# The expert stage of an attention and mixture-of-experts layer, with the weights as the stationary operand

## Chip, core and metric

The kernel runs on one core of one Trainium2 chip. The metric is the device time of one execution in microseconds (us). The core's engines work side by side, each through a queue of its own in program order: TensorE (PE in the profile; its weight loads are the row PEld), VectorE (DVE), ScalarE (ACT), GpSimd (POOL) and SyncE (SP), which here only issues transfers (DMAs). They wait for one another by semaphores alone. On TensorE a matmul streams the columns of its moving operand past a stationary operand, which a weight load puts in place ahead of it. `order` rows below name the output, then `<-`, the stationary or first input and the moving one.

## What is computed

The input x is 2 sequences of 2048 tokens of 256 numbers, 4096 tokens in all.

```python
def reference(x, Wq, Wk, Wv, Wo, Wg, bg, gate_w, ew1, ew2, ew3, sw1, sw2, sw3):
    x = x + layernorm(attention(layernorm(x)))       # gated linear attention, 16 heads of 16, a scan over time
    x = x + layernorm(ffn(layernorm(x)))
    return x

def ffn(x):
    top_v, top_i = top_k(x @ gate_w, 2)              # 8 experts, each token takes 2
    w = softmax of the two chosen gates, 0 elsewhere
    out = sum over experts e of swiglu(x, ew1[e], ew2[e], ew3[e]) * w[e]
    return out + swiglu(x, sw1, sw2, sw3)            # the shared expert

def swiglu(x, w1, w2, w3):                           # w1, w2: 256 x 512; w3: 512 x 256
    h = x @ w1
    return h * sigmoid(h) * (x @ w2) @ w3
```

## The kernel before

There are three parts. The **first stage** (functions `sync_a`, `tensor_a`, `vector_a`, `scalar_a`, `pool_a`) goes through the tokens in C = 16 steps of 128 tokens of both sequences: attention, the first residual (kept in DRAM as `x1_scratch`), the second norm (`xn2`) and the routing. Every step POOL scatters the rows of `xn2` four times over (2 sequences, 2 choices) by indirect DMA (`scatter`, L538 to L544) into `xs_scratch`, where each expert has a region of its own; SP also stores them in the tokens' order behind those regions (`store_xn2`, L348). The scales of the norms are made on POOL in `rstd_x`, `rstd_o` and `rstd_x1` (L516 to L535, with `ve` from the variances `mv`, `mvo`), which stand in POOL's queue among the scatters.

The **expert stage** works on tiles of 128 rows, in this order: EARLY = 12 tiles of the shared expert (which need no routing), RT = 72 routed tiles (8192 rows, and up to one part-filled tile for each of 8 experts), and 20 shared ones, the tail. Which expert a routed tile belongs to is known only on the chip: DVE writes it to a table, `tab`, and each engine loads the number of the expert from there into a register (`expert_of`, L1131; `entry`, L1128 and L1129). A weight's address is then worked out from this register. Everything is fp32 made of two f16 numbers, a high and a low part: a product is three f16 matmuls, high by high, high by low and low by high. With `xh`, `xl` for the rows, `gh`, `gl` for the gated hidden values, and `W16` for the weights.

Within a tile (`tensor_b`): `turn_x` (L1193) transposes the rows that SP loaded (`xt`); ACT makes `xh` (`high`, L1264), DVE `xl` (L1414). `hidden` (L1208) multiplies: the rows are stationary, the weights move, 512 columns at a time, 6 matmuls for `bank` of the first and 6 for the second product. ACT takes the silu (`sl`, L1270), DVE gates it (`gg`, L1425). `turn_g` (L1199) transposes `gg` in four pieces of 128x128 fp32; ACT and DVE make `gh` (L1258) and `gl` (L1407) of it. `project` (L1218) multiplies it by the down weights in 12 matmuls of 256 columns; ACT scales the result out (`yo` or `ysh`, L1282). SP stores `yo` in the order of the tiles in `ys_scratch` (L1145 to L1170). Engines run the three steps of a tile on slots that overlap: in slot t TensorE does `hidden` of tile t, the transposes of t-1 and t+1, and the down product of t-2.

**Weights.** The f32 weights of the experts arrive by DMA; DVE takes the largest absolute value of each (`largest_of`, L1350), beside the first slots (the list `beside`: a "table stage" is one entry of it), `scales` (L766) makes `w_scale` from them, and POOL then splits a whole expert in three instructions (`split` in `pool_b`: L1441, L1445, L1447) of 3072 elements a partition. Experts 0 to HEAD-1 are handled early; the others, seven of the nine with the shared one, in this way.

**Tail.** When all routed tiles are stored, POOL gathers for each step of 128 tokens of both sequences the routed results of each token (`gather`, L1475: four indirect DMAs, with `gi` copied at L1469); DVE mixes them with `ysh` by the gate's weights (`mix`: L1367, L1373; statistics at L1378 to L1387), POOL raises the variance to the power -1/2 (`rstd`, L1481), DVE makes the shift (L1393), ACT normalises (`lnc`, L1290), DVE adds x1 (`residual`), SP stores. POOL's part of this is `pool_c`, a queue of its own order: scale of step c, then gathers of c+2.

## Time and profile before

| what | us |
|---|---|
| device time, median of 3 runs (lowest to highest) | 885.7 (880.39 to 886.43) |
| the profiled execution's own time | 884.06 |
| its span on the core | 881.7 |
| TensorE busy | 779.2 (88% of the span) |
| TensorE's weight loads busy | 551.0 |
| DVE, ACT, POOL busy | 559.7, 423.7, 413.8 |
| DMA: packets, MB | 71381, 96.55 |

The span is the time from the first to the last instruction of the profiled execution, and the 2.4 us to its own time lie around it. Busy times are sums over the whole span; since the kernel has stages with other limits, they are read stage by stage, by windows and by the timeline. The page's "chain that ended last" is followed back from the last instruction to what released each. The page's course of three engines in 40 slices of 22 us (tenths of busy time; PEclk is TensorE's granted clock):

```
PE   3879888898999984899999999999999999977772
DVE  4797988897988993699433334433334433477774
POOL 3122335876777775681899960000000000377773
PEclk8899989999999997799999999999999999999996
```

The first stage takes the first 15 slices or so, the early shared tiles three more, the routed ones go on to slice 33, and the tail follows.

### The profile page before, as it was taken

Reading aid. Unit: us, or ns where it says so; the run is one execution under the profiler, and the core shown is the slowest. Engines: PE = TensorE matmul, PEld = TensorE weight load, DVE = VectorE, ACT = ScalarE, POOL = GpSimd, SP = SyncE. Lnnn points to the kernel's source line nnn. Section 1 sums busy time; section 2 is a strip of 40 time slices with the busy share of each in tenths; the row PEclk is TensorE's granted clock in tenths of the full one; section 3 lists DMA queues with packets and bytes.
Section 4 is the critical chain, followed back from the end, with each engine's and each line's share of the span. In section 5 each row is a group of like instructions: output and inputs, shape, how many; then the busy total and the mean of one; then the engine's idle time right before and its main releaser. Section 6 shows DMA issues by size and latency. Waiting matters only on the chain.

```text
span 881.7 us, 24476 instructions
## 1 busy us (share of the span) xinstructions
PE 779.2 (88%) x8205; PEld 551.0 (62%) x8205; DVE 559.7 (63%) x1195; ACT 423.7 (48%) x811; POOL 413.8 (47%) x452
## 2 busy tenths in 40 slices
PE   3879888898999984899999999999999999977772
PEld 3667667687877763466666666666666666644441
DVE  4797988897988993699433334433334433477774
ACT  2555556565666552343444444444444444444442
POOL 3122335876777775681899960000000000377773
PEclk8899989999999997799999999999999999999996
DMA  7243333443345347781111111111111212345554
GB/s 238 68 102 83 98 101 78 141 121 110 111 138 144 111 121 264 271 287 48 44 60 56 62 58 58 61 58 59 60 55 61 61 60 63 96 131 186 168 156 130
DMA packets 71381, 96.55 MB, mean 109 GB/s; under 512 B 8800, under 2 KB 58080, under 8 KB 71264
## 3 DMA queue, kind: packets, MB, share of 16 engines
q1 hardware_dynamic: 59376, 69.31, 26.5%
q0 software_dynamic: 6528, 17.83, 6.2%
q10 hardware_dynamic: 5360, 7.87, 2.7%
q8 instruction: 71, 1.16, 0.6%
q14 instruction: 46, 0.38, 0.1%
HBM read 63.25 MB, written 31.72 MB: 108 GB/s over the span
## 4 chain that ended last, share of the span: by engine, by line
PE 44%; DMA 5%; DVE 4%; issue 4%; POOL 3%; ACT 0%; POOLq 0%; SPq 0%; ACTq 0%; DVEq 0%
PE bank L1208 25%; PE bank L1218 12%; DMA ya<-ys_scratch,gi 4%; PE bank L1199 4%; PE bank L1193 2%; POOL ya L1475 2%; DVE cmb L1367 1%; DVE cmb L1373 1%; DVE stc L1378 0%; POOL xs_scratch L544 0%; DVE mvc L1384 0%; DMA xt<-xs_scratch 0%; POOL rsc L1481 0%; DVE vec L1387 0%; PE bank L741 0%
## 5 line engine op out<-in xcount | busy, mean ns | idle before, releaser
L1208 PE MATMUL bank<-W,xh 128*128 (+1 forms) x832 | 249.4, 382 | 15.3 <-DVE xl L1414 15.1
L1407 DVE TENSOR_TENSOR gl<-bank,gh 128x512 f16<-128x512 f32 x104 | 71.7, 690 | 162.9 <-ACT gh L1258 162.8
L1208 PE MATMUL bank<-W,xl 128*128 (+1 forms) x416 | 158.5, 381 | 0.0
L1218 PE MATMUL bank<-W,gh 128*128 (+1 forms) x832 | 143.4, 274 | 0.0
L1208 PEld LDWEIGHTS bank<-W,xh 128*128 128x128 f16 x832 | 80.4, 98 | 73.6 <-DVE xl L1414 19.7
L1218 PE MATMUL bank<-W,gl 128*128 (+1 forms) x416 | 114.1, 274 | 0.0
L1425 DVE SCALAR_TENSOR_TENSOR gg<-sl,w_scale,bank 128x512 f32<-128x512 f32 x104 | 77.6, 747 | 56.1 <-PE bank L1208 52.1
L1469 POOL COPY gi<-pos_all 128x4 uint32 (+1 forms) x16 | 2.9, 179 | 232.4 <-DMA ys_scratch<-yo 232.4
L544 POOL DMA_INDIRECT xs_scratch<-xn,posi x64 | 94.3, 1473 | 31.8 <-issue 23.2
L1218 PEld LDWEIGHTS bank<-W,gh 128*128 128x128 f16 x832 | 81.9, 98 | 31.8
L600 PE MATMUL bank<-xnT,wT 128*128 128x256 f32 x384 | 94.8, 399 | 0.7 <-ACT xnT L386 0.7
L1282 ACT ACTIVATE yo<-bank,w_scale 128x256 f32<-128x256 f32 x72 | 34.2, 475 | 126.3 <-PE bank L1218 126.3
L1258 ACT ACTIVATE gh<-bank 128x512 f16<-128x512 f32 x104 | 62.1, 597 | 57.4 <-PE bank L1199 57.4
L600 PEld LDWEIGHTS bank<-xnT,wT 128*128 128x128 f32 x384 | 73.0, 197 | 17.7 <-issue 5.9
L1270 ACT ACTIVATE sl<-bank,w_scale 128x512 f32<-128x512 f32 x104 | 71.5, 688 | 20.1 <-PE bank L1208 19.7
L1475 POOL DMA_INDIRECT ya<-ys_scratch,gi x64 | 67.5, 1055 | 27.0 <-POOL gi L1469 12.3
L834 DVE TENSOR_TENSOR_SCAN W<-W,diag 128x1024 f32<-128x1024 f32 x32 | 71.9, 2279 | 8.4 <-DMA W<-gate_scratch 8.3
L1199 PE MATMUL bank<-ident,gg 128*128 128x128 f32 x416 | 63.1, 274 | 14.2 <-DVE gg L1425 14.2
L1199 PEld LDWEIGHTS bank<-ident,gg 128*128 128x128 f32 x416 | 50.4, 141 | 39.2 <-issue 19.5
L1208 PEld LDWEIGHTS bank<-W,xl 128*128 128x128 f16 x416 | 40.9, 98 | 49.6 <-issue 1.1
L1441 POOL TENSOR_TENSOR wtmp_p<-W,w_scale 128x3072 f32<-128x3072 f32 x8 | 42.5, 5309 | 21.3 <-DVE w_scale L778 20.8
L704 PE MATMUL bank<-W 64*32 64x64 f32 x2048 | 35.3, 221 | 17.5 <-issue 13.8
(177 smaller groups left out, 1325.8 us busy)
## 6 DMA issues: line engine op xcount, KB each, us to landing
W<-gate_scratch SPq DMA_DIRECT2D x64, 256.0 KB, 4.8
xt<-xs_scratch SPq DMA_DIRECT2D x104, 128.0 KB, 2.0
ys_scratch<-yo SPq DMA_DIRECT2D x72, 128.0 KB, 1.7
W<-in_L_ffn_ew_dram ACTq DMA_DIRECT2D x15, 512.0 KB, 6.3
W<-in_L_ffn_ew_dram SPq DMA_DIRECT2D x9, 512.0 KB, 8.3
x_in<-in_L_attn_x_dram SPq DMA_DIRECT2D x16, 256.0 KB, 4.0
x_scratch<-x SPq DMA_DIRECT2D x16, 256.0 KB, 2.2
xs_scratch<-xn SPq DMA_DIRECT2D x16, 256.0 KB, 3.1
```

The costliest lines, as they stand in the source:

```text
L544: pool.indirect_dma_start(xs_d[:, :], bass.IndirectOffsetOnAxis(ap=posi[:, s, b * TOPK + k:b * TOPK + k + 1], axis=0), xn2[s % XB][:, b, : ...
L600: last = mm(dst[:, g * B * P:(g + 1) * B * P], wT[:, n, k, g * P:(g + 1) * P], xnT[s % 2][:, k, :], start=(k == 0), stop=(k == KC - 1))
L834: V.tensor_tensor_scan(dec[:, w, :], gbc[s % 2][:, w, :], free2(diag[:, :, :]), 0.0, ALU.mult, ALU.add).then_inc(S["decay_ready"], 1)
L1199: last = nc.tensor.transpose(pGT[:, c * P:(c + 1) * P], gg[t.side][:, c * P:(c + 1) * P], ident[:, :])
L1208: last = mm(dst[t.side][:, :], a[t.side][:, k, :], W16[:, e, m, s, k * H:(k + 1) * H], start=(n == 0), stop=(n == 3 * KC - 1))
L1218: last = mm(pYB[t.side][:, 0:D], a[t.side][:, c, :], W16[:, e, 2, s, c * D:(c + 1) * D], start=(n == 0), stop=(n == 3 * HC - 1))
L1258: act.activation(gh[u.side][:, :, :].rearrange("p c t -> p (c t)"), pGT[:, :], ACT.Copy)\
L1270: act.activation(sl[t.side][:, :], pH1[t.side][:, :], ACT.Silu, scale=w_scale[:, 0, e])\
L1407: V.tensor_tensor(gl[u.side][:, :, :].rearrange("p c t -> p (c t)"), pGT[:, :], gh[u.side][:, :, :].rearrange("p c t -> p (c t)"), ALU.sub ...
L1425: V.scalar_tensor_tensor(gg[t.side][:, :], sl[t.side][:, :], w_scale[:, 1, e], pH2[t.side][:, :], ALU.mult, ALU.mult).then_inc(T["gg_ready ...
L1441: pool.tensor_tensor(wtmp_p[:, :, :].rearrange("p m n -> p (m n)"), whole, w_scale[:, 1, e:e + 1].broadcast_to([P, 3 * MW]), ALU.mult).the ...
L1475: pool.indirect_dma_start(ya[c.side][b][k][:, :], None, ys_d[:, :], bass.IndirectOffsetOnAxis(ap=gi[c.side][:, b * TOPK + k:b * TOPK + k + ...
```

## The change

The expert stage is turned round. The weights are stationary and the rows move (`hidden`): a weight block of 128x128 meets the transposed rows of a **unit** of 256 rows. The hidden values come out transposed already, so the transposes of `gg` go (`turn_g`), and ACT and DVE take `gh` and `gl` from `gg` itself. The down product stays as it was, 12 matmuls of 256 columns for 128 rows and all of the hidden values.

A unit of 256 rows is worked through in two **halves**, each with half of the hidden columns (24 matmuls of 256 columns in `hidden`) and two chunks of the down product for its two tiles (12 matmuls of 256 columns); each half fills a slot. There are 6 early shared units (slots 0 to 11), PAIRS = 25 routed units of 256 rows (slots 12 to 61), and 21 routed **single** units of 128 rows for the rest (slots 62 to 82), each with 48 matmuls of 128 columns in `hidden`, 12 of 256 for the down product and 2 transposes. The tail begins at slot 83 with 10 shared units. RU = 46 is the number of routed units. The units of 256 rows take the first 25 full pairs of tiles in the experts' order; all other rows go to singles.

- **Shared rows.** SP stores the transposed `xn2T` of the first stage in `xT_scratch` (`store_xn2T`) in place of the rows, and the shared units load it transposed: no `turn_x` there.
- **Rows carry their destination.** A row of `xs_scratch` is DR = 272 floats, 1088 bytes: 256 of data, and the token's number and first choice, which POOL writes ahead of each step's scatters (two operations on 128x2 and a wait, `tagged`). POOL has seven more constants to make at the start. On DVE `rows_to` makes from them the row of `ys_scratch` that each result belongs to (`idx`).
- **Scatter in place of gather.** Results of routed units leave ACT into `yo` (3 buffers) and POOL scatters them to the tokens' order (`spread`, one indirect DMA for each 128 rows). `ys_scratch` is then in the tokens' order, and SP loads it for the tail with direct DMAs, two slots ahead (`load_mix`). The four gathers a step go.
- **POOL's queue.** It works slot by slot with the others: from slot SHARE + 1 = 11 on two thirds of an expert's split (`split(e, m)`, 1024 elements instead of 3072) a slot for four slots, then one, and behind them in each slot the scatter of the routed unit that ended three slots before. In the tail it takes over `low_g` (`gl`) in each slot, `low` (`xl`) every second one, and `residual`, beside the scale.
- **ACT and DVE** follow the new slots; the table stages beside the tiles on DVE are one fewer (`SHARE`).

The core of the diff:

```diff
-    EARLY = 12
-    T0 = EARLY + RT
...
+    EARLY = 6
+    PAIRS = -(-(TOPK * TOK - E * (2 * P - 1)) // (2 * P))
+    RU = PAIRS + (TOPK * TOK + E * (P - 1)) // P - 2 * PAIRS
...
-        xs_d = nc.dram_tensor("xs_scratch", [ROWS, D], F32).ap()
-        ys_d = nc.dram_tensor("ys_scratch", [RT * P, D], F32).ap()
+        xs_d = nc.dram_tensor("xs_scratch", [SPARE + P, DR], F32).ap()
+        ys_d = nc.dram_tensor("ys_scratch", [TOPK * TOK + (RU - PAIRS) * P, D], F32).ap()
+        xT_d = nc.dram_tensor("xT_scratch", [C, P, KC * B * P], F32).ap()
...
-            def store_xn2(s):
-                need(sp, S["xn2_ready"], B * (s + 1))
-                sp.dma_start(xs_by_step[s], xn2[s % XB][:, :, :]).then_inc(xs_stored[s % XB], 16)
+            def store_xn2T(s):
+                need(sp, S["xn2T_ready"], s + 1)
+                sp.dma_start(xT_d[s], free2(xn2T[s % 2][:, :, :])).then_inc(xT_stored[s % 2], 16)
...
             def scatter(s):
                 need(pool, S["pos_ready"], s // BATCH + 1)
                 need(pool, S["xn2_ready"], B * (s + 1))
+                need_dma(pool, scattered, s - XB, B * TOPK)
+                pool.tensor_scalar(xn2[s % XB][:, :, D], token2[:, :], float(TOPK * P * s), None, ALU.add)\
+                    .then_inc(tagged, 1)
+                pool.tensor_copy(xn2[s % XB][:, :, D + 1], choice_all[:, s, 0:B * TOPK:TOPK]).then_inc(tagged, 1)
+                need(pool, tagged, XB + 2 * (s + 1))
...
+        T2 = 2 * P
+        XT, SX, XH, GH_, YO, IDX, YA = 3, 4, 3, 3, 3, 8, 4
...
+        for kind, n in kinds:
+            tiles = 1 if kind == "routed" and n >= PAIRS else 2
+            first = len(halves)
+            units.append(unit(len(units), kind, n, tiles, tiles, first, first + tiles - 1))
+            for part in range(tiles):
+                per = HC // tiles
+                halves.append(half(len(halves), units[-1], part, range(part * per, (part + 1) * per), tiles * P))
+        NH = len(halves)
...
+        TAIL = units[EARLY + RU].first
+        mix_slot = [max(TAIL + 5 + c, TAIL + 2 * (c - EARLY) + 4) for c in range(C)]
...
+            def load_mix(c):
+                if c == 0:
+                    for r in range(RU - YO, RU):
+                        need_spread(sp, r)
...
+                sp.dma_start(ya[c % YA], ys_by_step[c]).then_inc(ya_loaded[c % YA], 16)
+                sp.dma_start(x1c[:, c], x1_by_step[c]).then_inc(x1_loaded[c % YA], 16)
...
+            def rows_to(u, e):
...
+                at = idx[u.n % IDX][:, 0:u.tiles]
+                if u.tiles == 2:
+                    V.scalar_tensor_tensor(at, xt[u.n % XT][:, 0:2, D + 1], eidx[:, e], xt[u.n % XT][:, 0:2, D],
+                                           ALU.not_equal, ALU.add).then_inc(T["idx_ready"], 1)
...
-            def turn_g(t):
-                due(pe, T["gg_ready"], 1, t, 1)
-                for c in range(HC):
-                    last = nc.tensor.transpose(pGT[:, c * P:(c + 1) * P], gg[t.side][:, c * P:(c + 1) * P], ident[:, :])
-                last.then_inc(T["ggT_done"], 1)
...
+            def hidden(x, e, m, dst, done):
+                a = x.u.i % XH
+                for ci, c in enumerate(x.chunks):
+                    cols = slice(ci * x.width, (ci + 1) * x.width)
+                    n = 0
+                    for k in range(KC):
+                        for s, src in ((0, xh), (0, xl), (1, xh)):
+                            last = mm(dst[x.h % 2][:, cols], W16[:, e, m, s, k * H + c * P:k * H + (c + 1) * P],
+                                      src[a][:, k, 0:x.width], start=(n == 0), stop=(n == 3 * KC - 1))
+                            n += 1
+                last.then_inc(T[done], 1)
...
-                for k in range(KC):
-                    if k == 1 and between is not None:
-                        between()
-                    for a, s in ((xh, 0), (xh, 1), (xl, 0)):
-                        last = mm(dst[t.side][:, :], a[t.side][:, k, :],
-                                  W16[:, e, m, s, k * H:(k + 1) * H], start=(n == 0), stop=(n == 3 * KC - 1))
-                        n += 1
-                last.then_inc(T[done], 1)
...
+            def rows_out(u, e):
+                need(act, T["y_done"], u.last + 1)
+                if u.kind == "shared":
+                    dst = ysh[:, u.n, :, :].rearrange("p b d -> p (b d)")
+                else:
+                    need_spread(act, u.n - YO)
+                    dst = free2(yo[u.n % YO][:, 0:u.tiles, :])
+                act.activation(dst, pYB[u.i % 2][:, 0:u.tiles * D], ACT.Copy, scale=w_scale[:, 2, e])\
+                   .then_inc(T["yo_ready"], 1)
...
+                if half_at(t - 1):
+                    high_g(half_at(t - 1))
+                if step_at(t - 1) is not None:
+                    norm(step_at(t - 1))
+                if t - 3 in ending:
+                    rows_out(ending[t - 3], experts[ending[t - 3].i])
+                x = half_at(t)
+                if x:
+                    if x.part == 0:
+                        experts[x.u.i] = expert_of(act, x.u)
+                    silu(x, experts[x.u.i])
+                if t + 2 in starting:
+                    high(starting[t + 2])
...
+            def split(e, m):
+                i = done[0]
+                done[0] += 1
+                need(pool, T["pool_split"], 3 * (i - 1))
+                pool.tensor_tensor(wtmp_p[i % 2][:, :], W[:, e, m, :], w_scale[:, 1, e:e + 1].broadcast_to([P, MW]),
...
+            def spread(u):
+                need(pool, T["yo_ready"], u.i + 1)
+                need(pool, T["idx_ready"], u.n + 1)
+                for j in range(u.tiles):
+                    settle(pool)
+                    pool.indirect_dma_start(ys_d[:, :], bass.IndirectOffsetOnAxis(
+                        ap=idx[u.n % IDX][:, j:j + 1], axis=0), yo[u.n % YO][:, j, :], None)\
+                        .then_inc(yo_spread[u.n % YO], 16)
...
-                for b in range(B):
-                    for k in range(TOPK):
-                        settle(pool)
-                        pool.indirect_dma_start(ya[c.side][b][k][:, :], None, ys_d[:, :], bass.IndirectOffsetOnAxis(
-                            ap=gi[c.side][:, b * TOPK + k:b * TOPK + k + 1], axis=0)).then_inc(ya_loaded[c.side], 16)
...
+            for t in SLOTS:
+                if t == SHARE + 1:
+                    pool.wait_ge(s_scale, 2)
+                if t > SHARE:
+                    for n in range(2 if t < SHARE + 5 else 1):
+                        if late_split:
+                            split(*late_split.pop(0))
+                if half_at(t - 1) and t - 1 >= TAIL:
+                    low_g(half_at(t - 1))
+                if t - 3 in ending and ending[t - 3].kind == "routed":
+                    spread(ending[t - 3])
+                if t + 2 in starting and is_tail(starting[t + 2]):
+                    low(starting[t + 2])
+                if step_at(t - 2) is not None:
+                    residual(step_at(t - 2))
+                if step_at(t) is not None:
+                    rstd(step_at(t))
 
```

How the change moves instructions is shown at three places. First TensorE's queue at a routed tile of before: the loads of the expert's numbers from the table, then the hidden product (ISA is a register instruction; matmul rows read output, moving operand, stationary operand and the moving size).

```order
L1129 TENSOR_LOAD tab
L1129 ISA x2
L1129 TENSOR_LOAD tab
L1129 ISA x2
L1208 ISA [waits b_xl_ready]
L1208 MATMUL bank1<-W,xh0 128x512
L1208 ISA
L1208 MATMUL bank1<-W,xh0 128x512
L1208 MATMUL bank1<-W,xl0 128x512
L1199 MATMUL bank5<-ident,gg1 128x128 [waits b_gg_ready,b_yo_ready]
L1199 MATMUL bank5<-ident,gg1 128x128 x3
L1193 MATMUL bank0<-ident,xt1 128x128 [waits xt_loaded1]
```

After, at the start of a single unit, with the expert's number and the hidden product:

```order
L1124 TENSOR_LOAD tab
L1124 ISA x2
L1227 ISA [waits b_silu_ready,b_xl_ready]
L1227 MATMUL bank1<-xh1,W 128x128
L1227 MATMUL bank1<-xl1,W 128x128
L1227 ISA
L1227 MATMUL bank1<-xh1,W 128x128
L1227 ISA
L1227 MATMUL bank1<-xh1,W 128x128
L1227 MATMUL bank1<-xl1,W 128x128
L1227 ISA
L1227 MATMUL bank1<-xh1,W 128x128
```

Before, 2 of 3 matmuls of 512 columns have a register instruction ahead of them, and the transposes of `gg` and `xt` stand between; now 2 of 3 matmuls of 128 columns have one, 32 of 48 in a single's hidden product, and nothing else stands there but the two transposes of the next unit's rows.

Second, POOL's queue where the last weights are split. Before, the three instructions of an expert, then the gathers:

```order
L1441 TENSOR_TENSOR wtmp_p<-W,w_scale 128x3072 [waits b_experts_split]
L1445 CAST W<-wtmp_p 128x3x1024 [waits b_pool_split]
L1447 TENSOR_TENSOR W<-wtmp_p,W 128x3x1024 [waits b_pool_split]
L1469 COPY gi0<-pos_all 128x4 [waits s_place,yo_stored0,yo_stored1]
L1475 DMA ya0_00<-ys_scratch,gi0 128x256 [waits c_gi_ready]
L1475 DMA ya0_01<-ys_scratch,gi0 128x256
L1475 DMA ya0_10<-ys_scratch,gi0 128x256
L1475 DMA ya0_11<-ys_scratch,gi0 128x256
L1469 COPY gi1<-pos_all 128x4
L1475 DMA ya1_00<-ys_scratch,gi1 128x256 [waits c_gi_ready]
```

After, the tenth third of the splits (`wtmp_p0`, `wtmp_p1` are the two halves of its buffer), with the scatter of routed unit 0, two more splits, and the scatter of unit 1:

```order
L1494 TENSOR_TENSOR wtmp_p0<-W,w_scale 128x1024 [waits b_pool_split]
L1498 CAST W<-wtmp_p0 128x1024 [waits b_pool_split]
L1500 TENSOR_TENSOR W<-wtmp_p0,W 128x1024 [waits b_pool_split]
L1511 DMA ys_scratch<-yo0,idx0 10880x256 [waits b_yo_ready,b_idx_ready]
L1511 DMA ys_scratch<-yo0,idx0 10880x256
L1494 TENSOR_TENSOR wtmp_p1<-W,w_scale 128x1024 [waits b_pool_split]
L1498 CAST W<-wtmp_p1 128x1024 [waits b_pool_split]
L1500 TENSOR_TENSOR W<-wtmp_p1,W 128x1024 [waits b_pool_split]
L1494 TENSOR_TENSOR wtmp_p0<-W,w_scale 128x1024 [waits b_pool_split]
L1498 CAST W<-wtmp_p0 128x1024 [waits b_pool_split]
L1500 TENSOR_TENSOR W<-wtmp_p0,W 128x1024 [waits b_pool_split]
L1511 DMA ys_scratch<-yo1,idx1 10880x256 [waits b_pool_split,b_yo_ready,b_idx_ready]
```

The scatters (L1511) now stand between the splits, two splits ahead of each.

Third, POOL's queue in the tail. Before, the scale of a step, then the gathers of the step two on:

```order
L1481 TENSOR_TENSOR rsc0<-vec0,half_neg 128x2 [waits c_vare]
L1469 COPY gi0<-pos_all 128x4 [waits ya_loaded0,c_mix2]
L1475 DMA ya0_00<-ys_scratch,gi0 128x256 [waits c_gi_ready]
L1475 DMA ya0_01<-ys_scratch,gi0 128x256
L1475 DMA ya0_10<-ys_scratch,gi0 128x256
L1475 DMA ya0_11<-ys_scratch,gi0 128x256
L1481 TENSOR_TENSOR rsc1<-vec1,half_neg 128x2 [waits c_vare]
```

After, two slots of the tail, the first with `low` (L1518), both with `low_g` (L1524), `residual` (L1537) and the scale (L1531):

```order
L1524 TENSOR_TENSOR gl0<-gg0,gh0 128x512 [waits b_y_done,b_gh_ready]
L1518 TENSOR_TENSOR xl0<-sx3,xh0 128x512 [waits b_up_done,b_xh_ready]
L1537 TENSOR_TENSOR W<-W 128x512 [waits x1_loaded1,c_lnc_ready]
L1531 TENSOR_TENSOR rsc1<-vec1,half_neg 128x2 [waits c_shift_ready,c_lnc_ready,c_vare]
L1524 TENSOR_TENSOR gl1<-gg1,gh1 128x512 [waits b_y_done,b_gh_ready]
L1537 TENSOR_TENSOR W<-W 128x512 [waits x1_loaded2,c_lnc_ready]
L1531 TENSOR_TENSOR rsc0<-vec0,half_neg 128x2 [waits c_shift_ready,c_lnc_ready,c_vare]
```

The gathers are gone, and ahead of each scale stand `low_g`, in every second slot `low`, and `residual`, each with its waits.

## Rows read from the trace of the kernel before

**Rows 1.** The page's part 4: the chain that ended last, by line.

```profile
PE bank L1208 25%; PE bank L1218 12%; DMA ya<-ys_scratch,gi 4%; PE bank L1199 4%; PE bank L1193 2%; POOL ya L1475 2%; DVE cmb L1367 1%; DVE cmb L1373 1%; DVE stc L1378 0%; POOL xs_scratch L544 0%; DVE mvc L1384 0%; DMA xt<-xs_scratch 0%; POOL rsc L1481 0%; DVE vec L1387 0%; PE bank L741 0%
```

**Rows 2.** Windows: busy us (instructions) of PE, PEld, DVE, ACT, POOL; clock, DMA share, GB/s.

```profile
250.00:300.00 50.00, 47.36 (x928) 37.94 (x926) 43.94 (x116) 31.80 (x60) 37.08 (x55) 1.00 0.41 120
...
500.00:600.00 100.00, 99.70 (x655) 66.16 (x654) 38.58 (x66) 44.86 (x88) 20.78 (x5) 1.00 0.19 59
780.00:800.00 20.00, 14.75 (x90) 8.62 (x90) 14.93 (x42) 8.92 (x18) 15.09 (x18) 1.00 0.56 164
```

**Rows 3.** Timeline of PE: start us, busy us, line, output<-inputs, count.

```profile
601.21 0.60 PE L1199 MATMUL bank<-ident,gg 128*128 128x128 f32 x4
601.65 0.38 PE L1193 MATMUL bank<-ident,xt 128*128 128x128 f32 x2
...
603.81 0.38 PE L1218 MATMUL bank<-W,gh 128*128 x2
...
605.12 0.59 PE L1208 MATMUL bank<-W,xh 128*128 x2
```

**Rows 4.** The chain that ended last in order of time: start us, us, what.

```profile
414.75 1.94 PE bank L1208 x9
...
743.23 1.94 PE bank L1208 x9
```

**Rows 5.** Timeline of POOL in the first stage; idle before and what ended it in brackets.

```profile
225.17 0.22 POOL L521 TENSOR_SCALAR ve<-mv 128x2 f32<-128x2 f32 x1 [0.92 <-DVE mv L810]
...
235.10 0.96 POOL L544 DMA_INDIRECT xs_scratch<-xn,posi  x1 [0.30 <-DVE mvo L810]
...
250.80 2.67 POOL L544 DMA_INDIRECT xs_scratch<-xn,posi  x1 [0.30 <-issue]
```

**Rows 6.** Timeline of PEld, TensorE's weight loads.

```profile
352.49 0.11 PEld L714 LDWEIGHTS bank<-before,ones 128*128 128x128 bf16 x1
352.52 0.13 PEld L764 LDWEIGHTS bank<-before,ones 128*128 128x128 bf16 x1
```

**Rows 7.** TensorE's queue, lines 1218 and 1129: ns min/median/max, first and last start.

```profile
L1218 PEldq FUSED_REGOPS  x8: 46/46/60, 561.4 to 562.3; - x8
...
L1129 PEldq TENSOR_LOAD <-tab x2: 299/300/302, 562.5 to 563.1; - x2
```

**Rows 8.** Timeline of POOL at an expert's weight split.

```profile
420.69 5.31 POOL L1441 TENSOR_TENSOR wtmp_p<-W,w_scale 128x3072 f32<-128x3072 f32 x1 [20.78 <-DVE w_scale L778]
...
428.95 6.03 POOL L1447 TENSOR_TENSOR W<-wtmp_p,W 128x3072 f16<-128x3072 f32 x1
435.06 5.31 POOL L1441 TENSOR_TENSOR wtmp_p<-W,w_scale 128x3072 f32<-128x3072 f32 x1
```

**Rows 9.** Groups by line and shape, POOL: busy us, mean ns, idle before.

```profile
L554 POOL TENSOR_TENSOR W<-qT,W 128x256 f32<-128x256 f32 x32 | 22.9, 735 | 12.7 <-DVE W L911 12.7
...
L563 POOL TENSOR_TENSOR x<-ln_o,x_in 128x512 f32<-128x512 f32 x16 | 20.8, 1298 | 15.1 <-ACT ln_o L380 15.1
L1481 POOL TENSOR_TENSOR rsc<-vec,half_neg 128x2 f32<-128x2 f32 x16 | 12.1, 755 | 11.1 <-DVE vec L1387 10.8
```

**Rows 10.** The chain that ended last, in the tail: start us, us, what.

```profile
804.23 4.04 DMA ya<-ys_scratch,gi
811.17 4.03 DMA ya<-ys_scratch,gi
```

**Rows 11.** Timeline of DVE in the tail.

```profile
768.71 0.88 DVE L1367 SCALAR_TENSOR_TENSOR cmb<-ya,wts_all,ysh 128x256 f32<-128x256 f32 x2
...
771.44 0.69 DVE L1407 TENSOR_TENSOR gl<-bank,gh 128x512 f16<-128x512 f32 x1
```

**Rows 12.** Timeline of ACT in the tail.

```profile
780.70 0.60 ACT L1258 ACTIVATE gh<-bank 128x512 f16<-128x512 f32 x1 [0.38 <-PE bank L1199]
...
781.57 0.69 ACT L1270 ACTIVATE sl<-bank,w_scale 128x512 f32<-128x512 f32 x1
...
785.70 1.09 ACT L1290 ACTIVATE lnc<-cmb,shiftc,rsc 128x256 f32<-128x256 f32 x2 [1.05 <-DVE shiftc L1393]
```

710 lines of the change are left out of this document (355 added, 355 removed).

## Prediction

> **What bounds the kernel now.** Start with the chain that ended last [rows 1]: 25% of the span is hidden matmuls, 12% down matmuls, 4% transposes of `gg`, 2% transposes of rows; the gathers of `ya` and DVE's mixing come behind. Then the windows [rows 2]: from 500 to 600 us TensorE is busy without a gap at clock 1.00; from 780 us on it is busy for 14.75 us of 20.
>
> Two marks carry the accounting. A tile's run of nine hidden matmuls starts 1.4 us behind the tile's start; the one at 414.75 is tile 12's (the first routed one) and that at 743.23 tile 84's (the first of the tail) [rows 4]: T12 = 413.3, T84 = 741.8, 328.5 us apart, 72 tiles of 4.56. The tail, 20 shared tiles and 16 mixing steps, takes 881.7 - 741.8 = 140 us.
>
> **Up to T12: +2.5 us.** Per step the change puts two operations on 128x2 (0.22 us, as `ve`) and a wait on Pool, some 0.7 us, ahead of the scatters; `rstd_o` stands behind these, and was already late for `mvo` once [rows 5]. Pool is busy for 37.1 of 50 us there [rows 2], which leaves some 4 a step, about 2 of it beyond the gaps between scatters. That covers most of it; I take 2.5, with 0 and 7 (0.7 for ten steps) as ends. The seven new constants stand beside the first weight loads. In the shared stage DVE keeps its seven maxima, one table stage earlier, with `gl`, `gg` and half a double `xl` each, as long as now; the tiles behind them go by TensorE. T12 moves by less than 0.5 us.
>
> **Routed stage, TensorE's array.** A matmul of 256 columns takes 1.31/12 = 0.109 us, an fp32 transpose 0.11 (four in 0.44), one of 512 columns 0.216 (nine and two transposes in 2.16) [rows 3]. A half of a pair is 24 + 12 matmuls of 256 columns, 3.92, and two row transposes, 0.22: 4.14 us against 4.56. The four transposes of `gg` are what goes. There are 50 such halves. A single is 48 matmuls of 128 columns, 12 of 256, two transposes. What 128 columns cost behind a load of 128x128 no row shows. Two 16-bit loads of 128x128 start 0.03 us apart [rows 6], so the load is not the bound, and half of 0.109 gives 0.055: 2.65 + 1.31 + 0.22 = 4.2 us.
>
> By the Trainium skill (TensorE: Matmul & The Clock Gate, Back-to-back issue gap) a stream of loads and matmuls at 128 columns takes about 81 ns each; the single would take 5.4 us. The page has 131 ns for 512 columns by the same measurement where this trace has 216, so I give it little weight.
>
> **Routed stage, TensorE's queue.** The expert's number is a register, and the order shows a register instruction (ISA) ahead of each new weight address. Eight start within 0.9 us, 0.129 apart; and a load of the number from the table takes 0.6 us [rows 7]. A tile of before has 16 and two loads: 3.3 us, hidden under 4.56. A pair half has 20 and half a load: 2.9, hidden under 4.14. A single has 32 ahead of its hidden matmuls, 8 ahead of the down ones, one load: 5.2 + 0.6 + 0.2 for its waits = 6.0 us, above 4.2. So the 21 singles take 126 us where the array alone would take 88. If 0.129 is not the queue's own price, 88 is the other end; at 0.14 it is 135.
>
> **Routed stage, Pool's queue.** Now the weight splits stand alone on Pool, 14.37 us an expert, from 420.69 us on [rows 8], long ahead of need. After the change ten of the 21 late splits (a third of an expert each) stand ahead of routed unit 0's scatter, then two ahead of each of the next five, one ahead of the seventh. 14.37/3 = 4.8 us, and six starts more per expert: 512 against 256 elements (1298 and 735 ns, [rows 9]) leave 0.17 for a start, so 4.8 + 6 x 0.17/3 = 5.1 us. A scatter takes 1.27 us (0.96 and 0.30, [rows 5]), a pair has two, and I give them 3 us to land (a gather's 4.04 from issue, less its 0.96, [rows 10]). The scales come some 3 us sooner (one table stage less): 418. The seventh pair leaves Pool at 418 + 21 x 5.1 + 7 x 2.53 = 542.8 and has landed at 546.
>
> `yo` has three buffers. ACT's `rows_out` of the fourth unit waits for the first scatter; behind it on ACT stand `silu` and `high`, for which TensorE waits two slots on. In this way the tenth pair (slot 34) waits for the seventh, and slot 36 starts at 546 + 0.6 + 0.7 + about 1 for its chain = 548. Undisturbed it would start at 413.3 + 24 x 4.14 = 512.7. Loss 35 us; 29 at 4.8 a split, 39 at 5.3. Behind the last split the scatters follow at once, so nothing more is lost.
>
> Routed stage: 50 x 4.14 + 35 + 126 = 368 us against 328.5: **+40**. Without both queues it would be 295, 33 less than now.
>
> **Tail.** Now Pool issues four gathers a step, and DVE waits for their landing; late steps are 6.9 us apart (804.23, 811.17, [rows 10]). Direct loads of rows that lie in the tokens' order replace them, two slots ahead and hidden by the slots. The new loop: DVE mixes 2.73 us (768.71 to 771.44, [rows 11]) and gates; Pool must have made the scale before the next shift. Ahead of that on Pool stand `low_g`, `residual` and, in every other slot, `low`: 1.3 us for 512 elements in f32 [rows 9], 1.15 for the two with an f16 output (a sixth of 6.03 and a start, [rows 8, 9]), and 0.75 for the scale's power on two [rows 9]. Without `low`, from the gate: `gh` 0.5 + 1.15 + 1.3 + 0.75 = 3.7, under TensorE's 3.92. With it: `low` waits for ACT's `high`, the last in ACT's slot, behind `gh`, the norm, the rows and the silu: 3.4 us (0.60, 1.09, 0.6, 0.69, 0.6 from [rows 12], the first half hidden); then 1.15 + 1.3 + 0.75: 6.7 us. Six slots of 3.92, six pairs of 3.8 + 6.7, one of 3.8: 90. From there gate, high, low, down and rows (5), the last mix (2.7), scale, shift, norm, sum and store (8): 105 us, **-35**. Ends: every slot at 3.92, 92; every Pool step a fifth longer, 115.
>
> **Sum.** 881.7 + 2.5 + 40 - 35 = 889 us of span, and 2.4 around it (884.06 less 881.7): 891.5. The profiled execution is 1.6 below the median of 885.7, and runs of before spread by 6. I take 890.
>
> **Rivals.**
> - *The register instructions hide.* If an address ahead of a weight load is worked out beside the matmuls, a single takes 4.2 us: -38, 852 us. For it: one shows only 46 ns as its own [rows 7]. Against: they stand 0.129 apart with one matmul between and with two. 0.19. (By the Trainium skill's 81 ns the single would be 5.4 us, and the time 877.)
> - *Pool doesn't hold TensorE.* If splits are quicker, or ACT's wait is covered by more than I count: -35, 855 us. For it: nothing of this kind waits in the trace of before. Against: ten splits are 48 us by any row, and the first waiting slot is 42 us behind T12. 0.06.
> - *Scatter rows of 1088 bytes cost double.* A scatter takes 0.96 us, and up to 2.67 in the first stage [rows 5]. If the 64 bytes beyond 1 KB double it, a step has 3.8 us more on Pool, 2 of them covered, for ten steps; and the 24 indirect DMAs behind the last step take 23 us more, by which expert 1's split and slot 12 are 20 late: +40, 930 us. It shows from 0.2 us more per scatter. 0.07.
> - My forecast, both queues binding and the tail at 5.2 us a slot: 0.68, with a range of its own of 873 to 906.
>
> **How the numbers follow.** In the forecast the singles give 118 to 133, the splits 29 to 39, the tail 92 to 115, the start 0 to 7. About 1% is what a measurement of this kernel can tell from no change: 876.8 to 894.6. An eighth of the 0.68 lies below (a short tail with quick splits), a quarter above. Faster 0.19 + 0.06 + 0.09 = 0.34; slower 0.07 + 0.17, and 0.02 for what I don't see, 0.26; same 0.40. The range takes in the first two rivals and the forecast: 850 to 905.
>
> **What the profile will show.** Pairs: matmuls of 256 columns 0.109 apart, and from 465 to 545 us TensorE idle for some 4 us in every 12.7 while Pool is full; ACT's `yo` waiting for a DMA from `yo` to `ys_scratch`. Singles: a period near 6.0, TensorE's idle put down to issue, eight register instructions per 1.03 us. Tail: no gathers, DVE's shift waiting for Pool by some 3 us in every other slot. I am wrong if a single takes 4.2 us, if ACT doesn't wait in slot 22, or if routed work starts later than 425.

## The result and the profile after

| | before | after |
|---|---|---|
| device time, median of 4 runs | 883.05 us | 933.0 us |
| lowest to highest | 876.64 to 886.43 | 929.35 to 939.03 |
| ratio, with its 95% interval | | 1.064 (1.059 to 1.069) |
| span of the profiled execution | 881.7 | 929.5 |

The change made the kernel 6.4% slower; 890 was forecast. The pages of after, first the busy times, two of the 40 slices' rows and the chain that ended last:

```profile
PE 769.3 (83%) x9439; PEld 635.9 (68%) x9439; DVE 580.0 (62%) x1178; ACT 404.6 (44%) x725; POOL 494.0 (53%) x583
...
PE   3889888999989848869926769999999999997751
...
POOL 4123337777876766839998984222221111446652
...
PE 28%; POOL 23%; issue 10%; DVE 2%; ACT 1%; DMA 1%; POOLq 0%; DVEq 0%; ACTq 0%; SPq 0%
PE bank L1227 18%; PE bank L1243 8%; POOL W L1500 6%; POOL wtmp_p L1494 5%; POOL W L1498 3%; POOL xs_scratch L527 2%; POOL W L1537 1%; POOL gl L1524 1%; PE bank L1216 1%; POOL ys_scratch L1511 1%; POOL rsc L1531 1%; POOL xs_scratch L563 1%; DMA ys_scratch<-yo,idx 0%; DMA xt<-xs_scratch 0%; DVE gg L1427 0%
```

Against [rows 1]: before, 43% of the span were matmuls and transposes of the expert stage. Now TensorE has 28% of the chain in all, and POOL, which had 3%, has 23%: 14% are its three split instructions (L1494, L1498, L1500). The windows, in the columns of [rows 2], say where:

```profile
420.00:440.00 20.00, 20.00 (x186) 18.02 (x184) 13.51 (x16) 8.78 (x14) 19.05 (x11) 1.00 0.06 15
460.00:480.00 20.00, 6.66 (x61) 5.72 (x59) 0.85 (x1) 0.00 (x0) 18.71 (x13) 0.77 0.04 13
480.00:500.00 20.00, 12.11 (x85) 9.74 (x86) 7.62 (x11) 6.76 (x11) 18.15 (x12) 0.76 0.09 28
600.00:620.00 20.00, 20.00 (x185) 18.01 (x184) 9.18 (x16) 8.82 (x14) 4.28 (x5) 1.00 0.23 69
740.00:760.00 20.00, 19.02 (x201) 14.83 (x200) 6.33 (x15) 6.86 (x14) 2.96 (x4) 1.00 0.16 49
860.00:880.00 20.00, 14.69 (x124) 11.30 (x123) 17.27 (x35) 9.77 (x18) 13.38 (x13) 1.00 0.55 172
```

From 460 us TensorE works 6.66 us of 20, then 12.11, with POOL at 18 to 19: this stretch, to 560 us, has no counterpart before. The granted clock is 0.77 and 0.76 in these two windows (0.85 to 0.89 up to 560), so part of what TensorE does between its waits runs at the lower of its two levels (1.2 GHz); POOL is the longer chain there. From 560 to 670 us TensorE is full, as it was from 500 to 600 [rows 2]. In the singles (740 to 760) it looks nearly full too, which misleads (below). In the tail it works 14.7 of 20 as before [rows 2], but now DVE is busy for 17 of 20 there, where it had 14.9.

The marks of the forecast, by the first hidden matmul of a slot: slot 12, the first routed one, starts at 416.71, the tail's slot 83 at 800.22.

| stretch | before | forecast | after |
|---|---|---|---|
| to the first routed matmul | 413.3 | 415.8 | 416.7 |
| routed stage | 328.5 | 368 | 383.5 |
| tail | 140 | 105 | 129.3 |

So of the 40 us between forecast and measurement 1 is at the start, 15 in the routed stage and 24 in the tail. In what follows a slot is marked by its silu on ACT (L1283), 1.6 us behind its first matmul: there are 103 of these, and they give the time of each slot.

### The profile page after: what moved, and what is told of

Read it like the earlier page. It is cut to its first block, busy times and chain, and to the rows that moved or that the text cites. A ratio compares the mean times of both kernels' runs of the same rounds, so it can differ in the third digit from the quotient of the medians.

```text
span 929.5 us, 26786 instructions
## 1 busy us (share of the span) xinstructions
PE 769.3 (83%) x9439; PEld 635.9 (68%) x9439; DVE 580.0 (62%) x1178; ACT 404.6 (44%) x725; POOL 494.0 (53%) x583
## 4 chain that ended last, share of the span: by engine, by line
PE 28%; POOL 23%; issue 10%; DVE 2%; ACT 1%; DMA 1%; POOLq 0%; DVEq 0%; ACTq 0%; SPq 0%
PE bank L1227 18%; PE bank L1243 8%; POOL W L1500 6%; POOL wtmp_p L1494 5%; POOL W L1498 3%; POOL xs_scratch L527 2%; POOL W L1537 1%; POOL gl L1524 1%; PE bank L1216 1%; POOL ys_scratch L1511 1%; POOL rsc L1531 1%; POOL xs_scratch L563 1%; DMA ys_scratch<-yo,idx 0%; DMA xt<-xs_scratch 0%; DVE gg L1427 0%
## 5 line engine op out<-in xcount | busy, mean ns | idle before, releaser
L1227 PE MATMUL bank<-xh,W 128*128 128x256 f16 (+1 forms) x1984 | 333.4, 262 | 59.0 <-DVE xl L1402 41.3
L1227 PEld LDWEIGHTS bank<-xh,W 128*128 (+1 forms) x1984 | 195.4, 99 | 103.8 <-issue 57.7
L1227 PE MATMUL bank<-xl,W 128*128 128x256 f16 (+1 forms) x992 | 256.2, 260 | 0.0
L1427 DVE SCALAR_TENSOR_TENSOR gg<-sl,w_scale,bank 128x512 f32<-128x512 f32 x103 | 76.7, 744 | 243.7 <-PE bank L1227 159.9
L1511 POOL DMA_INDIRECT ys_scratch<-yo,idx x71 | 69.1, 974 | 194.6 <-ACT yo L1298 181.4
L1289 ACT ACTIVATE gh<-gg 128x512 f16<-128x512 f32 x103 | 64.9, 630 | 185.2 <-DVE gg L1427 185.2
L1227 PEld LDWEIGHTS bank<-xl,W 128*128 (+1 forms) x992 | 99.0, 100 | 9.0
L1283 ACT ACTIVATE sl<-bank,w_scale 128x512 f32<-128x512 f32 x103 | 70.2, 682 | 79.8 <-PE bank L1227 79.5
L527 POOL DMA_INDIRECT xs_scratch<-xn,posi x64 | 89.5, 1398 | 27.5 <-issue 13.1
L1433 DVE TENSOR_TENSOR gl<-gg,gh 128x512 f16<-128x512 f32 x83 | 63.7, 767 | 18.4 <-ACT gh L1289 18.4
L1494 POOL TENSOR_TENSOR wtmp_p<-W,w_scale 128x1024 f32<-128x1024 f32 x24 | 50.2, 2092 | 16.4 <-DVE w_scale L763 15.6
L1298 ACT ACTIVATE yo<-bank,w_scale 128x512 f32<-128x512 f32 (+1 forms) x46 | 27.1, 589 | 68.3 <-DMA ys_scratch<-yo,idx 67.7
L1500 POOL TENSOR_TENSOR W<-wtmp_p,W 128x1024 f16<-128x1024 f32 x24 | 52.1, 2171 | 1.9
L1243 PEld LDWEIGHTS bank<-W,gl 128*128 128x128 f16 x412 | 40.7, 99 | 4.7
```

The source lines that it names most:

```text
L527: pool.indirect_dma_start(xs_d[:, :], bass.IndirectOffsetOnAxis(ap=posi[:, s, b * TOPK + k:b * TOPK + k + 1], axis=0), xn2[s % XB][:, b, : ...
L1227: last = mm(dst[x.h % 2][:, cols], W16[:, e, m, s, k * H + c * P:k * H + (c + 1) * P], src[a][:, k, 0:x.width], start=(n == 0), stop=(n == ...
L1243: last = mm(pYB[x.u.i % 2][:, j * D:(j + 1) * D], src[x.h % GH_][:, cols], W16[:, e, 2, s, c * D:(c + 1) * D], start=(x.part == 0 and n == 0),
L1283: act.activation(sl[x.h % 2][:, :], pH1[x.h % 2][:, :], ACT.Silu, scale=w_scale[:, 0, e])\
L1289: act.activation(gh[x.h % GH_][:, :], gg[x.h % 2][:, :], ACT.Copy).then_inc(T["gh_ready"], 1)
L1427: V.scalar_tensor_tensor(gg[x.h % 2][:, :], sl[x.h % 2][:, :], w_scale[:, 1, e], pH2[x.h % 2][:, :], ALU.mult, ALU.mult).then_inc(T["gg_re ...
```

## The experiments

The first two ask whether POOL's queue costs what the trace seems to say, the next two what bounds a single, then three take the tail apart, one the start, and the last three put together what helped.

### e1_paced: the splits at another pace

```diff
-                if t > SHARE:
-                    for n in range(2 if t < SHARE + 5 else 1):
-                        if late_split:
-                            split(*late_split.pop(0))
+                if late_split and t > SHARE and (t < SHARE + 5 or t % 2 == 0):
+                    split(*late_split.pop(0))
```

> The changed kernel, with POOL's late weight splits at another pace: one a slot in slots 11 to 14, then one in every second slot (before: two a slot, then one a slot). A pair of slots then holds one split of 5.24 us and two scatters of 2.5 us, 7.8 us of POOL, under TensorE's 8.3. Theory (the splits ahead of the scatters hold ACT's yo buffer, and so TensorE): the 47 us that slots 22 to 35 lose now go, some 886 us; ACT's yo no longer waits for a DMA. Rival (the landing of a scatter, 2.8 us, and the ring of three buffers are enough to hold ACT): at least half of the loss stays, 910 or more. Rival (one split a pair is too slow and TensorE waits for the weights): xt loads late, 900 to 930.

Measured: 887.56 us (before, on the same chip, 878.53; ratio 1.011, 1.005 to 1.018), a span of 884.3. The silu of slots 12 and 62 lie 207.4 us apart, 50 times 4.15; in the changed kernel it was 254.4. So 47.0 us were lost to the order of POOL's queue, and nothing else stands in that stretch. ACT's `yo` by line, first after, then e1_paced (last two figures: idle time before it, and what ended most of it):

```profile
L1298 ACT ACTIVATE yo<-bank,w_scale 128x512 f32<-128x512 f32 (+1 forms) x46 | 27.1, 589 | 68.3 <-DMA ys_scratch<-yo,idx 67.7
```

```profile
L1298 ACT ACTIVATE yo<-bank,w_scale 128x512 f32<-128x512 f32 (+1 forms) x46 | 27.1, 589 | 0.7
```

The wait for the scatters' DMA, 67.7 us on ACT, is gone. Both rivals are out.

### e2_ring6: six buffers in place of three

```diff
-        XT, SX, XH, GH_, YO, IDX, YA = 3, 4, 3, 3, 3, 8, 4
+        XT, SX, XH, GH_, YO, IDX, YA = 3, 4, 3, 3, 6, 12, 4
```

> The changed kernel with six yo buffers in place of three (and 12 idx buffers in place of 8), the pace of the splits as it is. Theory: a unit's rows_out waits for the scatter six units back and not three, so TensorE runs 3 x 8.3 = 25 us further before it is held by the same backlog: some 908 us, the first wait of ACT for a scatter in slot 28 and not in slot 22, and splits at the same times as before. Rival (something else than the buffers, the splits' own load on the memory for one, slows the stretch): 925 to 933.

Measured: 911.27 us (two runs), a span of 906.6. The first long gap between two silu comes ahead of slot 30 (8.3 us) and not ahead of 22; from slot 12 to 62 it takes 232.2 us, 22.2 less than with three buffers, against 25 expected, and in the steady part each pair of slots still takes 13.8 to 14.5 us, as with three. More buffers only let TensorE run on until the same backlog catches it. One thing was off: the first wait came in slot 30 and not in 28, for the first scatter had by then landed.

### e3_second and e4_static: what bounds a single

e3_second gives every matmul an address instruction of its own:

```diff
-                        experts[x.u.i] = expert_of(pe, x.u)
+                        experts[x.u.i] = expert_of(pe, x.u), expert_of(pe, x.u)
...
-                            last = mm(dst[x.h % 2][:, cols], W16[:, e, m, s,
+                            last = mm(dst[x.h % 2][:, cols], W16[:, e[1 if src is xl else 0], m, s,
```

> The changed kernel, where TensorE loads the number of the expert into a second register too, and takes the address of the third matmul of each group (low part of the rows, high part of the weights) from that one. So every matmul of routed work has an address instruction of its own: 48 + 12 in a single in place of 32 + 8, 24 + 6 in a half of a pair in place of 16 + 4, and one more table load a unit. Theory (a single is bound by TensorE's own queue, at 0.129 us an address): a single takes 60 x 0.129 + 1.2 + 0.2 = 9.1 us (6.14 now), a half of a pair 4.5 (4.15), together some 63 + 15 us more, about 1010 us. Rival (the addresses are worked out beside the matmuls, and a matmul of 128 columns behind a weight load costs more than the 0.055 that I gave it): no change, 933, or only the table loads, 945.

e4_static takes all of them away in the singles:

```diff
-                        experts[x.u.i] = expert_of(pe, x.u)
+                        experts[x.u.i] = bass.ds(1, 1) if x.u.tiles == 1 else expert_of(pe, x.u)
```

> The changed kernel, where TensorE takes expert 1's weights for all 21 single units, by a fixed address, so that no address instruction and no table load stands in its queue there; the results of the singles of the other experts are so not the reference's. Theory (queue-bound singles): a single takes the array's own 4.2 us, 41 us less in all, 892 us. By the Trainium skill (TensorE: Matmul & The Clock Gate, Back-to-back issue gap) a load and matmul of 128 columns take about 81 ns and the single 5.4 us: 917 us. Rival (the addresses cost nothing): 6.1 us a single and 933.

Measured, each in one run: 1017.74 us and 894.41 us, spans of 1016.0 and 892.6. From the silu of slot 62 to that of 83:

| | address instructions a single | 21 singles, us | one |
|---|---|---|---|
| e4_static | 0 | 87.9 | 4.19 |
| after | 40 and a table load | 129.0 | 6.14 |
| e3_second | 60 and two table loads | 194.4 | 9.26 |

With none of them the single takes what the array alone was forecast to take, 4.2. The step from 40 to 60 is 3.12 us; less 0.6 for the load [rows 7] that is 2.52 for 20, 0.126 each, the 0.129 of [rows 7]. The instructions don't hide. (The Trainium skill, TensorE: Matmul & The Clock Gate, Back-to-back issue gap, would have 81 ns for a load and matmul of 128 columns; the trace of e4_static has 48 of them, 12 of 256 columns and two transposes in 4.19 us, so 0.055 us each. Trace and page do not agree here.) Only the pair halves of e3_second miss the expectation: slots 38 to 62 take 117.4 us, 4.89 a half, not 4.5. The silu there follow at some 4.4 and 5.3 us in turn, and the longer one lies at the start of a unit, where both table loads stand: 30 addresses at 0.129, 1.2 for the loads and 0.2 for the waits are 5.3. The last of the 24, into the first single, is 6.9. The expectation had spread the loads over both halves. Why the other half takes 4.4 is open.

How this looks in a profile is worth a look. The timeline of TensorE within a single of the changed kernel, then of e4_static:

```profile
739.08 0.35 PE L1227 MATMUL bank<-xh,W 128*128 128x128 f16 x2
739.27 0.22 PE L1227 MATMUL bank<-xl,W 128*128 128x128 f16 x1
739.33 0.35 PE L1227 MATMUL bank<-xh,W 128*128 128x128 f16 x2
739.52 0.22 PE L1227 MATMUL bank<-xl,W 128*128 128x128 f16 x1
739.58 0.35 PE L1227 MATMUL bank<-xh,W 128*128 128x128 f16 x2
...
740.51 0.22 PE L1227 MATMUL bank<-xh,W 128*128 128x128 f16 x1
740.57 0.22 PE L1227 MATMUL bank<-xl,W 128*128 128x128 f16 x1
740.62 0.28 PE L1227 MATMUL bank<-xh,W 128*128 128x128 f16 x2
```

```profile
730.09 0.27 PE L1227 MATMUL bank<-xh,W 128*128 128x128 f16 x2
730.20 0.22 PE L1227 MATMUL bank<-xl,W 128*128 128x128 f16 x1
730.26 0.27 PE L1227 MATMUL bank<-xh,W 128*128 128x128 f16 x2
```

Every row has a busy time of about 0.22 for one matmul, and 0.27 to 0.35 for two, in both kernels. What differs is the start times: a group of three starts each 0.25 us after (739.08, 739.33, 739.58), which is two address instructions, and each 0.17 us in e4_static. The busy times overlap and fill the gaps, so that TensorE reads as busy for 19.0 of 20 us. Behind the two transposes (740.51 on) three matmuls start 0.055 apart, for the queue had time to run ahead. The queue's own rows, of L1227 in the changed kernel, give the same:

```profile
L1227 PEldq FUSED_REGOPS  x8: 46/46/46, 739.1 to 740.0; - x8
```

Eight start within 0.9 us, as in [rows 7], each with 46 ns of its own.

### e5_lowg, e6_resid, e7_scale: the tail

All three start from e1_paced, so they are read by the tail, from the silu of slot 83 to the end of the span: 127.8 us both in the changed kernel and in e1_paced. (They and e8_early8 ran on another chip, on which the kernel before took 908.48 us, so their medians say little against its 887.56; the tail is read inside one trace each.) What they move in the tail, in short:

```diff
 e5_lowg
-                if half_at(t - 1) and t - 1 < TAIL:      # DVE
+                if half_at(t - 1):
                     low_g(half_at(t - 1))
...
 e6_resid
+                if step_at(t - 2) is not None:           # DVE, behind gated; taken out of POOL
+                    residual(step_at(t - 2))
...
 e7_scale
+                if step_at(t) is not None:               # POOL
+                    rstd(step_at(t))
                 if step_at(t - 2) is not None:
                     residual(step_at(t - 2))
-                if step_at(t) is not None:
-                    rstd(step_at(t))
```

> e1_paced, with the tail's low_g (gl, 1.15 us on POOL) on DVE again (0.75 us there), in each of the 20 slots. Tail: from the silu of slot 83 to the end, 127.8 us in e1_paced; two slots take 12.15 us in its steady part, and there four DVE operations are longer by 0.94, 1.09, 0.89 and 0.67 us while POOL works on low_g, residual, low_g and low. Theory (an operation of DVE with its operands in SBUF stands still until POOL's is over): two of the four stretches go, 1.83 us, and 1.50 us of work comes to DVE: a pair of slots 11.8, the tail some 2 us shorter, 885 us; L1463 and L1445 back at 0.16 and 0.44 us each. Rival (POOL's own queue of operations ahead of the scale is the bound, as the forecast had it): 2 x 1.15 us a pair less, the tail 16 us shorter, 872.

> e1_paced, with the tail's residual (1.27 us on POOL) on DVE, behind the gate (0.69 us there). Theory (DVE stands still beside POOL): per pair of slots the stretch of 1.09 us at L1441 goes, and the scale no longer stands behind the residual (1.24 us of idle time of DVE), against 1.38 us of new work: about 1 us less a pair, the tail 6 us shorter, 881 us. Rival (no such hold, DVE's own work is the bound): 0 to 1.4 us more a pair, 887 to 896.

> e1_paced, with the scale (rstd) ahead of the residual in POOL's queue in each slot of the tail, nothing else. In the slots with low, DVE now idles 1.24 us for the scale, which stands behind low and the residual. That goes; the residual then lies beside DVE's shift and first mix instead, where it still holds them: 1.2 to 2 us less a pair of slots, the tail 7 to 12 us shorter, 876 to 881. Rival (DVE's stretched work is the bound, whatever the order): under 3 us, 885 or more.

| | median (runs) | span | tail | against e1_paced |
|---|---|---|---|---|
| e1_paced | 887.56 (4) | 884.3 | 127.8 | |
| e5_lowg | 886.53 (2) | 891.3 | 125.3 | -2.5 |
| e6_resid | 884.18 (2) | 882.6 | 114.9 | -12.9 |
| e7_scale | 886.83 (2) | 881.9 | 127.0 | -0.8 |

First the rows that led to the theory, POOL and DVE in the tail of the changed kernel:

```profile
841.90 1.15 POOL L1524 TENSOR_TENSOR gl<-gg,gh 128x512 f16<-128x512 f32 x1
841.97 1.10 DVE L1463 SCALAR_TENSOR_TENSOR shiftc<-mvc,rsc 128x2 f32<-128x2 f32 x1 [1.24 <-POOL rsc L1531]
...
842.99 1.97 DVE L1441 SCALAR_TENSOR_TENSOR W<-W,wts_all,ysh 128x256 f32<-128x256 f32 x2
843.01 1.27 POOL L1537 TENSOR_TENSOR W<-W 128x512 f32<-128x512 f32 x1
```

The shift (L1463) works on 128x2. It starts at 841.97, 0.07 behind POOL's `gl`, and ends at 843.07, when `gl` (841.90 and 1.15) ends. Then the two operations of L1441 begin beside POOL's residual at 843.01 and take 1.97 us. In the next slot, where POOL is idle, both take what they should:

```profile
847.72 0.16 DVE L1463 SCALAR_TENSOR_TENSOR shiftc<-mvc,rsc 128x2 f32<-128x2 f32 x1
...
847.83 0.88 DVE L1441 SCALAR_TENSOR_TENSOR W<-W,wts_all,ysh 128x256 f32<-128x256 f32 x2
```

An operation of DVE on two operands in SBUF thus stands still until POOL's is over. Two operands are not the whole rule, for the operation that readies the variance (L1458) has one, and is held too where `low` (L1518) runs:

```profile
838.89 1.16 POOL L1518 TENSOR_TENSOR xl<-sx,xh 128x512 f16<-128x512 f32 x1 [1.32 <-ACT xh L1277]
839.23 0.84 DVE L1458 TENSOR_SCALAR vec<-mvc 128x2 f32<-128x2 f32 x1
...
846.74 0.17 DVE L1458 TENSOR_SCALAR vec<-mvc 128x2 f32<-128x2 f32 x1
```

Where no `low` runs beside it, it takes the 0.17 us of the last row, while the aggregate of the statistics (L1455, one operand too) that runs beside the same `low` is no longer than elsewhere. Which operations of one operand are held was not tried further. By groups, L1441 and L1463 from 840 to 900 us (columns as in [rows 9]):

```profile
L1441 DVE SCALAR_TENSOR_TENSOR W<-W,wts_all,ysh 128x256 f32<-128x256 f32 x20 | 14.8, 782 | 2.1 <-ACT ysh L1298 2.1
...
L1463 DVE SCALAR_TENSOR_TENSOR shiftc<-mvc,rsc 128x2 f32<-128x2 f32 x10 | 6.3, 633 | 6.5 <-POOL rsc L1531 6.2
```

Before, the same operations of the tail took 0.484 and 0.160 us; with those of L1445 and L1458 it is 17.3 us more in ten slots, 1.7 a slot, of 6.07.

e5_lowg came out at 2.5 us, the 2 of the theory and not the rival's 16: 0.75 us of work a slot came to DVE, and about as much stretch left it. Here are the same two operations in e5_lowg and e6_resid, from 800 to 850 us:

```profile
L1438 DVE SCALAR_TENSOR_TENSOR W<-W,wts_all,ysh 128x256 f32<-128x256 f32 x18 | 7.9, 476 | 0.0
...
L1460 DVE SCALAR_TENSOR_TENSOR shiftc<-mvc,rsc 128x2 f32<-128x2 f32 x8 | 5.5, 686 | 5.2 <-POOL rsc L1528 5.0
```

```profile
L1441 DVE SCALAR_TENSOR_TENSOR W<-W,wts_all,ysh 128x256 f32<-128x256 f32 x20 | 17.7, 925 | 0.0
...
L1469 DVE SCALAR_TENSOR_TENSOR shiftc<-mvc,rsc 128x2 f32<-128x2 f32 x10 | 1.5, 150 | 0.0
```

In e5_lowg L1438 (the L1441 of after) is at 0.476 again, for it now lies beside no POOL operation, but the shift at 0.686 is not: for POOL's residual now begins 0.07 us ahead of it, in the place of `low_g` (829.59 and 829.66 in its timeline). In e6_resid the shift is at 0.150 and the first mix at 0.925, since now `low_g` lies beside it. Its gain is twice what I expected, and a pair takes 10.4 us (12.15 in e1_paced): the stretch of the shift, 0.48 us a slot, went too, which I had put down to `low_g` alone. e7_scale refuted my own account of its 1.24 us. The idle time went and came back as stretch. The row of the shift in e1_paced, then in e7_scale:

```profile
L1463 DVE SCALAR_TENSOR_TENSOR shiftc<-mvc,rsc 128x2 f32<-128x2 f32 x8 | 5.1, 634 | 5.2 <-POOL rsc L1531 5.0
```

```profile
L1463 DVE SCALAR_TENSOR_TENSOR shiftc<-mvc,rsc 128x2 f32<-128x2 f32 x9 | 11.0, 1219 | 0.9 <-POOL rsc L1531 0.7
```

Of 5.2 us of idle time 0.9 are left, but an operation takes 1.219 us and not 0.634. While POOL has as much to do beside DVE, its order does not matter; it only moves the place where DVE stands.

### e8_early8: more work ahead of the routed stage

```diff
-    EARLY = 6
+    EARLY = 8
```

> e1_paced with 8 early shared units in place of 6 (16 slots ahead of the routed ones), so 8 and not 10 in the tail. Theory: in e1_paced TensorE waits some 7.5 us in slot 10 for the rows of routed unit 0, which SP loads when POOL has split expert 1; four more early slots (4 x 4.1) cover that wait, so routed work starts 9 us later and not 16; the tail has two slots less and no unit beside the last four mixing steps: 15 to 20 us shorter. In all 6 to 11 us less, 876 to 881. Rival (the wait only moves, since POOL's splits or the routing are late for the routed units whenever these begin): 888 to 895.

Measured: 894.13 us (two runs), inside the rival's 888 to 895; a span of 893.8 and 9.5 more than e1_paced's, of which 4.5 lie ahead of the first slot. The first 16 slots took 74.3 us, where the first 12 of e1_paced took 61.3; so four more slots cost 13.0, and a gap of 5.9 stayed ahead of slot 13. The tail was 9.1 us shorter, not 15 to 20. It is no gain: the early slots cost more than the tail gives back, and e5_lowg, e6_resid and e7_scale had 884 to 887 us on the same chip.

### e10_stage and e11_stage_lowg: weights at a fixed place

```diff
+        hid = [as_weights(flat[:, (EARLY + 4 * n) * part:(EARLY + 4 * n + 4) * part], 2) for n in range(2)]
...
+                            w = W16[:, e, m, s] if single(x.u) is None else hid[single(x.u) % 2][:, m, s]
...
+                        V.tensor_copy(hid[i % 2].rearrange("p m s n -> p (m s n)"),
+                                      W16[:, experts[u.i], 0:2].rearrange("p e m s n -> p (e m s n)"))\
+                         .then_inc(T["hid_staged"], 1)
```

> e6_resid (paced splits, residual on DVE), and for the singles a fixed place for the weights: DVE copies the hidden weights of a single's expert (4096 f16 a partition) into one of two buffers, ACT the down weights (2048 f16) into one of three, in memory that is free there (rows of ysh that only the tail writes, and POOL's split buffers). Only these two copies take their address from a register; TensorE's 60 matmuls of a single have fixed addresses. Theory (queue-bound singles): as with the fixed weights of e4_static a single takes 4.2 us and not 6.14, if DVE (2.0 us a slot now) and ACT (2.0) have room for the copies: DVE at 0.25 ns an element 1.1 us, at 0.5 ns 2.1, at 1 ns 4.2 (then 6.2 a single, no gain); ACT at 0.85 ns 1.8 us. At 0.5 ns or less: 40 us less than e6_resid's 882.6 of span, 843. Rival: a copy is slower than that and the single stays at 5 to 6 us, 860 to 883.

> e10_stage with the tail's low_g on DVE too, so that POOL has only low and the scales there. In e6_resid a slot of the tail takes 5.2 us, DVE works without a gap, and its L1441 is stretched by 0.89 us a slot beside POOL's low_g. Theory (DVE stands still beside POOL): 0.75 us of new work against 0.89 of stretch, the tail 0 to 3 us shorter than e10_stage's. Rival (no hold): 0.75 us a slot more, the tail 12 us longer.

Measured: 831.28 us and 831.44, against 879.06 of before on the same chip; ratios 0.945 (0.940 to 0.950) and 0.946 (0.941 to 0.951). The 21 singles took 87.9 us, 4.19 each. The copies on DVE and ACT, from 640 to 710 us:

```profile
L1524 DVE COPY ysh<-W 128x4096 f16 x17 | 20.9, 1227 | 0.0
```

```profile
L1353 ACT ACTIVATE wtmp_p<-W 128x2048 f16 x12 | 22.8, 1900 | 0.0
```

DVE takes 0.30 ns an element (1227 ns for 4096), ACT 0.93. Both fit: in the window from 640 to 700 us TensorE works without a gap, DVE 46 us of 60 and ACT 52.

```profile
640.00:700.00 60.00, 60.00 (x887) 57.92 (x885) 46.12 (x87) 52.12 (x74) 16.11 (x15) 1.00 0.24 74
```

The tail is 114.1 us in e10_stage and 113.2 in e11_stage_lowg, 0.9 less, which is again the theory of the stretch and not 12 more. In time the two are the same.

### e12_rows_first: the rows ahead of the weights

```diff
-                sp.wait_ge(T["experts_split"], e)
-                settle(sp)
                 need(sp, T["xtT_done"], u.n - XT + 1)
...
                   .then_inc(xt_loaded[u.n % XT], 16)
+                sp.wait_ge(T["experts_split"], e)
+                settle(sp)
+                sp.sem_inc(T["weights_there"], 1)
```

> e11_stage_lowg, where SP loads the rows of a routed unit (xt) without a wait for the split of its expert's weights; behind the load SP waits for the split and tells TensorE and DVE by a semaphore of its own that the weights are there. In e11_stage_lowg the rows of unit 0 are loaded at 402.66, when POOL has split expert 1, and TensorE waits for them in slot 10, ahead of its transposes, 7.5 us (silu of slot 10 to slot 11 11.2 us, other slots 4.1 to 4.3). Theory (the start is late for that load alone): the rows come at 388, slots 10 and 11 run through, the silu of slot 12 comes 53 to 55 us behind that of slot 0 (61.0 now), all 6 to 7 us less, about 824. Rival (POOL's split of expert 1 is itself what slot 12 waits for): 2 us or less.

Measured: 825.97 us against 880.74, ratio 0.938 (0.934 to 0.943): 6.2% faster than before. From the silu of slot 0 to that of slot 12 it takes 53.2 us, as expected (61.0 in e11_stage_lowg). But part of it comes back at once: slot 13 starts 8.0 us behind slot 12, and up to slot 22 the gain is 4.7 us, which stays to the end (464.9 us from slot 0 on, 469.6 in e11_stage_lowg), short of the 6 to 7 expected. The chain there:

```profile
408.91 2.15 POOL W L1544
...
413.00 2.81 DMA largest_scratch<-wmax
415.82 3.58 DMA spread_b<-largest_scratch
...
422.37 0.70 DVE gl L1461
...
423.11 1.78 PE bank L1256 x12
```

Behind POOL's split of expert 1 (to 411.06) SP sends the largest weights to all partitions (two transfers of 2.81 and 3.58 us); DVE's next `gl` stands behind the scales made of them, and TensorE's down product waits for it. The wait for the split moved from one chain into another, which stands in the same queue of SP.

## Why the prediction was wrong, point by point

- **The sign and the mechanisms.** I had the routed stage longer, the tail shorter, and a time that hardly moves. Both queues that I named for the routed stage bind, and each was shown by taking it away: 47.0 us for POOL's splits (e1_paced), 41 for the address instructions and the table load (129.0 less 87.9, e4_static). The time went out of the range by two terms of the sum.
- **The term of the tail, -35, was the large miss (measured -11).** I put it together from POOL's own operations at the durations that they have alone, which they kept (`gl` 1.15 us, the residual 1.27), and took DVE's from [rows 11], where POOL made gathers beside it and nothing that DVE would have to wait for. I never asked what DVE's and POOL's operations do to each other when they lie side by side, though the change puts three new ones of POOL there. Nineteen slots, from the silu of slot 83 to that of 102, took 102.6 us where the sum has 90. Four operations of DVE (L1441, L1445, L1458, L1463) are stretched by 23.6 us in them; that is more than the 12 that are missing, for part of it takes the place of idle time, as e7_scale shows. In e11_stage_lowg, where POOL has only `low` and the scales, the same slots take 91.8 us, although DVE makes `gl` and the residual too: 11 of the 12 are back. That it is the hold that went, and not POOL's chain that got shorter, follows from e5_lowg (2.5 us and not 16) and e7_scale (another order, the same time). DVE, and not POOL's chain, was the bound. The Trainium skill has the rule (GPSIMD Engine Reference, Key points: POOL shares its way into SBUF with VectorE and contends, among others, with operations that have two SBUF inputs); the trace agrees, with the shift at 1.10 us beside `gl` and 0.16 without.
- **The other half of the tail's miss lies behind the last slot.** From the silu of slot 102 to the end the sum has 15.7 us (5, 2.7 and 8), and it took 25.2; another 1.5 is the start of the tail, from the first matmul to the silu, which the sum doesn't count. The sum has one mixing step there. Two follow one another, and the last rows of the shared expert wait for the first of them:

```profile
912.29 1.09 ACT L1305 ACTIVATE W<-W,shiftc,rsc 128x256 f32<-128x256 f32 x2 [5.29 <-DVE shiftc L1463]
913.29 0.67 ACT L1298 ACTIVATE ysh<-bank,w_scale 128x512 f32<-128x512 f32 x1
```

  TensorE ended its last down product at 909.2, but in ACT's queue the rows (L1298) stand behind the norm of the step before (L1305), which waits 5.29 us for its shift. So DVE's last mix starts at 914.05, 9.7 us behind the silu and not 5, and from it to the end are 15.5 us and not 10.7. e11_stage_lowg has 21.4 in place of the 25.2, so the hold is about 4 of it; no run took the order of ACT's queue apart.
- **The backlog of POOL, +35 (measured +47).** The mechanism, the place (slot 22, then each pair to slot 34) and the order were as forecast. A split was mis-sized: the first ten took 5.74 us each (419.43 to 476.79) and not 5.1. Here are one beside DVE's work and one while DVE waits:

```profile
430.89 2.42 POOL L1494 TENSOR_TENSOR wtmp_p<-W,w_scale 128x1024 f32<-128x1024 f32 x1
433.44 1.04 POOL L1498 CAST W<-wtmp_p 128x1024 f16<-128x1024 f32 x1
434.56 2.45 POOL L1500 TENSOR_TENSOR W<-wtmp_p,W 128x1024 f16<-128x1024 f32 x1
...
479.10 1.91 POOL L1494 TENSOR_TENSOR wtmp_p<-W,w_scale 128x1024 f32<-128x1024 f32 x1
481.14 1.04 POOL L1498 CAST W<-wtmp_p 128x1024 f16<-128x1024 f32 x1
482.26 2.13 POOL L1500 TENSOR_TENSOR W<-wtmp_p,W 128x1024 f16<-128x1024 f32 x1
```

  The second takes 5.24 us, close to the 5.1. The first takes 6.3, by the same contention seen from the other side. The seventh pair's last scatter landed at 559.8 and not at 546.
- **The singles, 6.0 us each (measured 6.14).** Right, with its working: e3_second and e4_static gave 0.126 us an address and 4.19 us without. One sign that I promised was wrong: TensorE's wait is not put down to issue, it does not show as a wait at all.
- **The array: 4.14 us a half of a pair (measured 4.15).** Right.
- **The start, +2.5 (measured +3.4).** The size was nearly right, the reason not. I had POOL's new operations delay the first stage, but the first slot's silu, which ends that stage, comes at 356.1 in the changed kernel and at 360.4 before, and in the other runs of it shown here between 354.5 and 367.6: a term of 2.5 cannot be seen there. What delays routed work is a wait that I left out: TensorE is through with its early slots sooner, since they are shorter, and stands in slot 10 for rows that SP loads only when POOL has split expert 1 (402.57 to 414.30 between two silu). e12_rows_first took 7.8 us of it away, and 4.7 stayed.
- **The rivals.** That register instructions hide, and that POOL doesn't hold TensorE, both fell. That the scatters cost double fell too, though its 930 us is the time that came out: a scatter of 1088 bytes took 1398 ns in the mean, and before one of 1024 took 1473:

```profile
L527 POOL DMA_INDIRECT xs_scratch<-xn,posi x64 | 89.5, 1398 | 27.5 <-issue 13.1 <-POOL xn L522 12.9 <-DVE mvo L795 1.5
```

  A time that agrees with a rival is no evidence for it.

What stays open: why the second half of a pair in e3_second takes 4.4 us, why the early slots of e8_early8 took as long as they did, and the share of each cause behind the last slot. None was tried further.

## What to carry to other kernels

Where a change gives work to POOL beside DVE, price both at what they take side by side: look for a stretch of the trace in which they meet, for the time that either takes alone says too little. In a queue that serves both a backlog without haste and results that others wait for, give the backlog the pace at which it is needed (here one split a unit), and check what stands behind it. And where addresses come from registers, count them: a busy TensorE at small matmuls may be one that waits for its own queue, and a copy to a fixed place by an idle engine pays for itself. At the end of a kernel, count the steps that are left to follow one another, and look what the last one waits for in each queue.

## What the runs showed of the hardware that I had not expected

- DVE's operation of 128x2 took 1.10 us beside one of POOL, and 0.16 alone; POOL's split instructions went from 1.89, 1.04 and 2.12 us to 2.42, 1.38 and 2.45 beside DVE. The gate (`gg`, L1427), which has one operand in PSUM, was not held: 0.73 us from 839.99 on, beside POOL's residual. An operation with one operand, in SBUF (L1458), was: 0.84 us beside `low`, 0.17 alone.
- An address instruction on TensorE costs 0.126 us of its queue and shows 46 ns. Matmuls of 128 columns with a weight load each started 0.055 us apart when nothing stood between them.
- DVE copied 4096 f16 numbers a partition in 1.227 us, 0.30 ns each, ACT 2048 in 1.90 us.
